# Second self-attention of a Perceiver block: products of whole 128-token tiles, or of 32 by 32 blocks

## The chip, the cores and the metric

The kernel runs on one core of one Trainium2 chip. The metric is the device time of one execution in microseconds. The program is straight-line code for five engines, which meet through semaphores: PE (matmul), DVE (vector), ACT (scalar), POOL (GpSimd) and SP, which issues most of the DMAs.

## The reference, cut to what matters

Six stages follow each other on x of shape (32 batches, 32 tokens, 256 channels): cross-attention, a compressed self-attention with a Fourier transform, a mixture of experts, and the same three once more with other formulas. The change touches stage five, the second self-attention. It has no weights; q, k and v are all the layer-normed x:

```python
def _L1_attn_ref(x):
    qkv = x.reshape(B, S, H, hd).transpose(0, 2, 1, 3)      # H = 16 heads of hd = 16
    q = k = v = qkv
    w = jnp.einsum('bhqd,bhkd->bhqk', q, k) / jnp.sqrt(jnp.asarray(hd, x.dtype))
    w = jnp.where(causal[None, None, :, :], w, mask_value)
    w = jax.nn.softmax(w, axis=-1)
    return jnp.einsum('bhqk,bhkd->bhqd', w, v).transpose(0, 2, 1, 3).reshape(B, S, D)
x = x + _L1_attn_ref(_layernorm(x, axis=-1))
```

A token attends to the tokens of its own batch up to itself, 32 at most.

## The kernel before

The 1024 tokens are eight tiles (`NT`) of 128 partitions, and a tile holds four batches (`QB`) of 32 tokens (`T`). For the self-attention the layer norm (L1459) writes into `xpad`, where each head has 32 columns (`PAD`): its 16 channels, a column of ones, and 15 zeros, which POOL sets ahead (L2098, L2099). Because q and k are the same, the product matrix of a head is symmetric.

For tile n the engines do this. PE transposes xpad, four transposes of four heads (`turn`, L960), into one PSUM bank (t % 2). ACT (even tiles, L1355) or DVE (odd tiles, L1771) copies it to `xpadT`, where head 4r+g is at partitions 32g to 32g+31, block r. PE multiplies each head's 32 x 128 slice with itself (`products`, L973): 16 matmuls, 128 keys by 128 tokens, into the four banks of `upper`, one bank for each g. ACT exponentiates a bank at a time into `gram` (L1365, four instructions). DVE multiplies the pieces g = 0 and 2, and POOL the pieces 1 and 3, by `keep`, which is one where key and token are of the same batch and the key isn't later (L1793, L2106): three quarters of each matrix are other batches' products, set to zero here. PE weighs (`weigh`, L983): 16 matmuls over all 128 keys, with xpad as the stationary operand, which gives channels by tokens in bank 2; the column of ones gives the sum of the exponentials. ACT copies that to `gout` (L1372), PE transposes it back into bank 3 (`turn_back`, L992), and DVE takes the reciprocal of the sums (L1778), scales (L1779), adds to x (L1782) and takes the statistics for the next layer norm (L1437).

The order on each engine is the order of the text; there is no planner. PE's loop is: turn(n+2), products(n+1), turn_back(n-1), weigh(n). `gram`, `gout` and `mixed` have two buffers each, `upper` has one, banks 2 and 3 one each. `after(engine, semaphore, value)` is a wait that is left out for values up to zero.

The stage is written out for all eight tiles, without a loop at run time. The cross-attention before it has one (`slots`, L524): its eight slots are repeated. After the stage, `ln(5)` and `turn_xn(5)` (L574) prepare the experts, whose router matmuls are L1015; the weights of the experts are fetched once the routing is known (L452 to L456).

A float32 matmul shows in the profile as two loads of the stationary operand (PEld) and two MATMULs (PE); a transpose as one of each.

Of the kernel before, what the change touches and what calls it, by code (L numbers as in the profile page):

```python
# [44 lines left out]
C_IDENT, C_SAME, C_PAIR, C_HM1, C_HM16 = 0, 128, 160, 162, 170  # L45
C_CS, C_BD, C_KEEP, C_EVEN, C_RQ, C_RK = 178, 1202, 1458, 1586, 1588, 1620
C_IOTA = C_RK + 32 * (KW2 + 1)
# [15 lines left out]
HG = 3  # L63
KQ = QB * NKEY

V_BQ, V_BK, V_BV, V_CB, V_BO, V_NK, V_NV = 0, 2, 4, 6, 8, 10, 12
# [3 lines left out]
def shape_constants():  # L70
# [21 lines left out]
    q = (p % T)[:, None]  # L92
    c[:, C_KEEP:C_KEEP + P] = (p[:, None] // T == p[None] // T) & (p[:, None] <= p[None])

# [45 lines left out]
def perceiver_block(nc, io, out):  # L140
    ctx = ExitStack()
    with ctx:
# [203 lines left out]
        xpadT = ar.take(GH, TOK)  # L346
        gram = [[ar.take(GH, P) for _ in range(2)] for _ in range(4)]
        gout = [ar.take(GH, P) for _ in range(2)]
        mixed = [ar.take(NH, HD) for _ in range(2)]
        keep = const[:, C_KEEP:C_KEEP + P]  # L350

# [212 lines left out]
        def _(pe):  # L564
# [383 lines left out]
            def self_gram():  # L948
                q = selfs[1]

                def turn(t):

                    if t >= NT:
                        return
                    pe.wait_ge(ln_norm, 4 * NT + t + 1)
                    if t == 0:
                        pe.wait_ge(q["pads"], 1)
                    after(pe, q["turnc" if t % 2 == 0 else "turnd"], t // 2)
                    for r in range(GH):
                        ins = nc.tensor.transpose(bank[t % 2][:, r * P:r * P + P],  # L960
                                                  xpad[:, t, 4 * r:4 * r + 4, :].rearrange("p h d -> p (h d)"), ident)
                    ins.then_inc(q["turnw"], 1)

                def products(n):

                    if n >= NT:
                        return
                    pe.wait_ge(q["turnc" if n % 2 == 0 else "turnd"], n // 2 + 1)
                    after(pe, q["exp"], 4 * n)
                    for r in range(GH):  # L970
                        for g in range(4):
                            v = xpadT[PAD * g:PAD * g + PAD, r, n * P:n * P + P]
                            ins = mm(upper[:, g, r * P:r * P + P], v, v, start=True, stop=True)  # L973
                    ins.then_inc(q["sw"], 1)

                def weigh(n):

                    pe.wait_ge(q["keptv"], 2 * n + 2)
                    pe.wait_ge(q["keptg"], 2 * n + 2)
                    after(pe, q["outc"], n)  # L980
                    for r in range(GH):
                        for g in range(4):
                            ins = mm(bank[2][PAD * g:PAD * g + PAD, r * P:r * P + P], xpad[:, n, 4 * r + g, :],  # L983
                                     gram[g][n % 2][:, r, :], start=True, stop=True)
                    ins.then_inc(q["pvw"], 1)

                def turn_back(n):

                    pe.wait_ge(q["outc"], n + 1)
                    after(pe, q["normed"], n)  # L990
                    for r in range(GH):
                        ins = nc.tensor.transpose(bank[3][:, r * P:r * P + P], gout[n % 2][:, r, :], ident)  # L992
                    ins.then_inc(q["backw"], 1)

                turn(0)
                turn(1)
                products(0)
                for n in range(NT):
                    turn(n + 2)
                    products(n + 1)  # L1000
                    if n:
                        turn_back(n - 1)
                    weigh(n)
                turn_back(NT - 1)

# [103 lines left out]
        def _(act):  # L1109
# [237 lines left out]
            def self_gram():  # L1347
# [9 lines left out]

                def exps(n, g):

                    if n >= NT:  # L1360
                        return
                    act.wait_ge(q["sw"], n + 1)
                    after(act, q["pvw"], n - 1)

                    A(gram[g][n % 2].rearrange("p r q -> p (r q)"), upper[:, g, :], ACT.Exp, scale=HD ** -0.5)\  # L1365
                        .then_inc(q["exp"], 1)

                def weighed(n):

                    act.wait_ge(q["pvw"], n + 1)  # L1370
                    after(act, q["backw"], n - 1)
                    A(gout[n % 2].rearrange("p r q -> p (r q)"), bank[2][:, :], copy).then_inc(q["outc"], 1)  # L1372

                turned(0)
                for g in range(4):
                    exps(0, g)
                for n in range(NT):
                    if n % 2 == 0:
                        turned(n + 2)
                    for g in range(4):  # L1380
                        exps(n + 1, g)
                    weighed(n)

# [43 lines left out]
        def _(dve):  # L1427
# [335 lines left out]
            def self_gram():  # L1763
                q = selfs[1]

                def turned(t):

                    if t >= NT:
                        return
                    dve.wait_ge(q["turnw"], t + 1)  # L1770
                    V.tensor_copy(xpadT[:, :, t * P:t * P + P], bank[t % 2][:, :].rearrange("p (r q) -> p r q", q=P))\  # L1771
                     .then_inc(q["turnd"], 1)

                def norm(n):

                    dve.wait_ge(q["backw"], n + 1)
                    o = bank[3][:, :].rearrange("p (h e) -> p h e", e=PAD)
                    mine(V.reciprocal(srcp[:, :], o[:, :, HD]))  # L1778
# [8 lines left out]

                turned(1)
                for n in range(NT):
                    for g in (0, 2):  # L1790
                        dve.wait_ge(q["exp"], 4 * n + g + 1)
                        v = gram[g][n % 2]
                        V.tensor_tensor(v, v, keep.unsqueeze(1).to_broadcast([P, GH, P]), ALU.mult).then_inc(q["keptv"], 1)  # L1793
                    if n % 2 == 0:
                        turned(n + 3)
                    if n:
                        norm(n - 1)
# [171 lines left out]
        def _(pool):  # L1969
# [125 lines left out]
            def self_gram():  # L2095
# [79 lines left out]
```

## Time and profile before

| | us |
|---|---|
| median of 3 runs (lowest, highest) | 1092.13 (1090.56, 1094.88) |
| the profiled execution, its own time | 1092.83 |
| its span | 1091.0 |
| PE busy / PEld busy | 938.4 / 757.0 |
| DVE / ACT / POOL busy | 548.6 / 466.8 / 340.6 |
| mean granted clock of PE | 0.924 |

The span runs from the first to the last instruction. PE is the matmuls, PEld the weight loads, which overlap them. The page cuts the span into 40 slices of 27 us; the second self-attention lies in slices 32 and 33 counted from 1 (859.9 to 905.1 us). The granted clock is 1.0 at 2.4 GHz and 0.5 at 1.2 GHz.

### The profile page before, as it was taken

Reading aid. Unit: us, or ns where it says so; the run is one execution under the profiler, and the core shown is the slowest. Engines: PE = TensorE matmul, PEld = TensorE weight load, DVE = VectorE, ACT = ScalarE, POOL = GpSimd, SP = SyncE. Lnnn points to the kernel's source line nnn. Section 1 sums busy time; section 2 is a strip of 40 time slices with the busy share of each in tenths; the row PEclk is TensorE's granted clock in tenths of the full one; section 3 lists DMA queues with packets and bytes.
Section 4 is the critical chain, followed back from the end, with each engine's and each line's share of the span. In section 5 each row is a group of like instructions: output and inputs, shape, how many; then the busy total and the mean of one; then the engine's idle time right before and its main releaser. Section 6 shows DMA issues by size and latency. Waiting matters only on the chain.

```text
span 1091.0 us, 24374 instructions
## 1 busy us (share of the span) xinstructions
PE 938.4 (86%) x8690; PEld 757.0 (69%) x8690; DVE 548.6 (50%) x1690; ACT 466.8 (43%) x1374; POOL 340.6 (31%) x388
## 2 busy tenths in 40 slices
PE   5899999979888679999996688999988674799993
PEld 3677777744465469999985466777766453699993
DVE  3666565540264621111117779777776475333334
ACT  2677677742322222332323376777766452011110
POOL 2321112000110141111122468878885250511111
PEclk9899999988898689999996799999999787899997
DMA  8211118000000089888835011111000000899984
GB/s 252 77 40 41 41 39 249 22 1 1 0 1 1 25 304 336 324 323 325 336 120 176 1 40 40 41 41 40 0 1 2 2 2 1 296 322 341 332 324 131
DMA packets 49155, 136.03 MB, mean 125 GB/s; under 512 B 15976, under 2 KB 35696, under 8 KB 43056
## 3 DMA queue, kind: packets, MB, share of 16 engines
q1 hardware_dynamic: 45328, 124.67, 33.0%
q0 software_dynamic: 3744, 10.26, 2.5%
q8 instruction: 51, 0.84, 0.3%
q14 instruction: 32, 0.26, 0.1%
HBM read 117.54 MB, written 17.38 MB: 124 GB/s over the span
## 4 chain that ended last, share of the span: by engine, by line
PE 66%; DVE 16%; POOL 6%; issue 5%; DMA 3%; ACT 2%; SPq 2%; DVEq 0%; POOLq 0%; ACTq 0%
PE lower L1065 14%; PE upper L1076 11%; PE upper L631 7%; PE upper L660 7%; PE upper L696 5%; POOL xslot L2117 3%; PE lower L682 3%; PE upper L713 3%; PE upper L838 2%; PE upper L733 1%; DVE x L1950 1%; PE upper L642 1%; POOL arena L1987 1%; PE lower L883 1%; SPq L428 1%
## 5 line engine op out<-in xcount | busy, mean ns | idle before, releaser
L1065 PEld LDWEIGHTS lower<-arena 128*128 128x128 f32 x1472 | 171.7, 192 | 6.3 <-issue 2.2
L1065 PE MATMUL lower<-arena 128*128 128x128 f32 x1472 | 172.6, 276 | 2.6 <-DMA arena<-in_b_dram 1.2
L1076 PE MATMUL upper<-arena 128*128 128x256 f32 x552 | 130.5, 388 | 0.0
L2123 POOL DMA_INDIRECT ytok<-arena,dest x46 | 44.0, 957 | 257.2 <-DVE arena L1912 235.6
L660 PE MATMUL upper<-wkv,arena 128*128 128x256 f32 x512 | 121.5, 379 | 0.0
L1076 PEld LDWEIGHTS upper<-arena 128*128 128x128 f32 x552 | 104.3, 195 | 13.0
L660 PEld LDWEIGHTS upper<-wkv,arena 128*128 128x128 f32 x512 | 94.3, 191 | 11.3
L1404 ACT ACTIVATE arena<-lower,arena 128x128 f32<-128x128 f32 x184 | 52.5, 369 | 114.2 <-PE lower L1065 114.2
L696 PE MATMUL upper<-const,arena 128*128 128x128 f32 x512 | 80.1, 279 | 6.4 <-ACT arena L1209 6.2
L631 PE MATMUL upper<-wkv,arena 128*128 128x256 f32 x256 | 73.1, 421 | 8.2 <-ACT arena L1146 4.5
L696 PEld LDWEIGHTS upper<-const,arena 128*128 128x128 f32 x512 | 59.6, 142 | 28.2 <-issue 12.6
L2019 POOL TENSOR_TENSOR arena<-arena 128x512 f32<-128x512 f32 x64 | 67.6, 1068 | 14.3 <-DMA arena<-in_ctxT_dram 14.2
L1199 ACT ACTIVATE arena<-arena 128x257 f32<-128x257 f32 x128 | 63.2, 498 | 2.4 <-DVE arena L1486 2.4
L2025 POOL TENSOR_TENSOR arena<-qT,const 128x256 f32<-128x256 f32 x32 | 22.9, 720 | 130.3 <-PE lower L682 114.0
L631 PE MATMUL upper<-arena,wkv 128*128 128x257 f32 x256 | 62.7, 389 | 0.6 <-ACT vlast L1132 0.6
L1410 ACT ACTIVATE arena<-lower 128x512 f32<-128x512 f32 x23 | 13.7, 597 | 114.0 <-PE lower L1065 114.0
L631 PEld LDWEIGHTS upper<-wkv,arena 128*128 128x128 f32 x256 | 49.5, 208 | 17.5 <-ACT arena L1146 4.9
L1199 ACT ACTIVATE arena<-lower,arena 128x257 f32<-128x257 f32 x128 | 59.0, 480 | 5.8 <-DVE arena L1488 5.8
L1900 DVE COPY arena<-lower 128x256 f32<-128x256 f32 x42 | 17.7, 420 | 85.1 <-PE lower L1049 85.1
L2117 POOL DMA_INDIRECT xslot<-arena,slot x32 | 31.9, 996 | 90.6 <-DVE tile_expert L1881 54.9
L1912 DVE COPY arena<-upper 128x256 f32<-128x256 f32 x46 | 19.5, 425 | 74.7 <-PE upper L1076 74.7
L1515 DVE TENSOR_TENSOR arena<-upper,arena 128x128 f32<-128x128 f32 x64 | 18.5, 289 | 75.4 <-ACT arena L1217 75.4
(250 smaller groups left out, 1763.0 us busy)
## 6 DMA issues: line engine op xcount, KB each, us to landing
arena<-in_ew_dram SPq DMA_DIRECT2D x23, 2048.0 KB
arena<-in_ew_dram SPq DMA_DIRECT2D x23, 1536.0 KB
arena<-in_ctxT_dram SPq DMA_DIRECT2D x16, 1028.0 KB, 5.1
xslot<-zero SPq DMA_DIRECT2D x2, 2967.0 KB, 18.8
arena<-xslot SPq DMA_DIRECT2D x46, 129.0 KB
xn<-ytok SPq DMA_DIRECT2D x8, 256.0 KB, 3.9
outT<-ytok SPq DMA_DIRECT2D x8, 256.0 KB, 4.7
const<-in_const_dram SPq DMA_DIRECT2D x1, 1158.0 KB, 7.6
```

The lines of the kernel that those rows point to most:

```text
L631: ins = mm(o, a, v, start=(c == 0), stop=(c == KC - 1))
L660: ins = mm(bank[6 + w][:, 0:D], dctx[k2][:, c, j2, w * P:w * P + P], wkv[l][:, c, D:2 * D], start=(c == 0), stop=(c == KC - 1))
L682: ins = mm(bank[i][64 * c:64 * c + 64, 0:S], xq[k2][rows, c, j2, :, :].rearrange("p e q -> p (e q)"), ktb[j2 % 2][rows, c, :], start=True, ...
L696: ins = nc.tensor.transpose(bank[4][:, i * P:i * P + P], prob[j % 2][:, i, w * P:w * P + P], ident)
L713: mm(bank[5][32 * i:32 * i + 32, 64 * c:64 * c + 64], vb[j % 2][:, w, c * P + 32 * i:c * P + 32 * i + 32], probT[j % 2][:, w, i, 64 * c:64 ...
L1065: ins = mm(bank[1 + half][:, i * P:i * P + P], ew[k][:, at:at + P], exT[k % 2][:, c, :], start=(c == 0), stop=(c == KC - 1))
L1076: ins = mm(bank[4 + k % 2][:, 0:D], eh[k % 2][:, i, :], ew[k][:, at:at + D], start=(i == 0), stop=(i == nh - 1))
L1199: A(prob[j2 % 2][:, i, :], src, ACT.Exp, bias=negmax[j2 % 2][:, i:i + 1], accum_out=rowsum[j2 % 2][:, i:i + 1]).then_inc(q["probs"], 1)
L1404: ins = A(eh[k % 2][:, c, :], bank[1 + half][:, i * P:i * P + P], ACT.Gelu_apprx_tanh, bias=eb1[k][:, c:c + 1])
L2019: G.tensor_tensor(dctx[k2][:, :, j2, :], of[:, :, 0:LASTKEY], of[:, :, LASTKEY:S].to_broadcast([P, KC, LASTKEY]), ALU.subtract).then_inc(q ...
L2117: G.indirect_dma_start(out=xslot[l], out_offset=at(i, t), in_=xrow[:, t, :], in_offset=None)\
L2123: G.indirect_dma_start(out=ytok[l], out_offset=bass.IndirectOffsetOnAxis(ap=dest[k][:, 0:1], axis=0), in_=eys[k], in_offset=None).then_inc ...
```

## The change

Products are made for a batch's own 32 by 32 block only, so that a head and a batch are one matmul with 32 rows and 32 columns of the array; row group g and column group b are the tile of the array that it uses. All 16 heads' blocks of a tile of tokens are 128 partitions by 512 elements, in the first 128 columns of the four banks. One exponential and one mask product take them all, and the mask only has to be causal (32 columns wide). The weighing has the exponentials as stationary operand and xpad as the moving one, 17 columns (`HW`), with head h of batch b at partitions 32b of bank 2 + n % 2: keys are summed and tokens come out on the partitions, so that the copy and the transpose back are gone. ACT makes all copies of the transposes; POOL has no part in the tiles.

```diff
-C_CS, C_BD, C_KEEP, C_EVEN, C_RQ, C_RK = 178, 1202, 1458, 1586, 1588, 1620
+C_CS, C_BD, C_KEEP, C_EVEN, C_RQ, C_RK = 178, 1202, 1458, 1490, 1492, 1524
...
+HW = HD + 1
...
-    c[:, C_KEEP:C_KEEP + P] = (p[:, None] // T == p[None] // T) & (p[:, None] <= p[None])
+    c[:, C_KEEP:C_KEEP + T] = q <= np.arange(T)[None]
...
-        gram = [[ar.take(GH, P) for _ in range(2)] for _ in range(4)]
-        gout = [ar.take(GH, P) for _ in range(2)]
+        gram = [ar.take(4, GH, T) for _ in range(2)]
...
 # PE
-                    after(pe, q["turnc" if t % 2 == 0 else "turnd"], t // 2)
+                    after(pe, q["turnc"], t - 1)
...
-                    after(pe, q["exp"], 4 * n)
+                    pe.wait_ge(q["turnc"], n + 1)
+                    after(pe, q["exp"], n)
                     for r in range(GH):
                         for g in range(4):
-                            v = xpadT[PAD * g:PAD * g + PAD, r, n * P:n * P + P]
-                            ins = mm(upper[:, g, r * P:r * P + P], v, v, start=True, stop=True)
+                            for b in range(QB):
+                                v = xpadT[PAD * g:PAD * g + PAD, r, n * P + T * b:n * P + T * b + T]
+                                ins = mm(upper[T * b:T * b + T, g, T * r:T * r + T], v, v, start=True, stop=True)
                     ins.then_inc(q["sw"], 1)
 
                 def weigh(n):
-                    pe.wait_ge(q["keptv"], 2 * n + 2)
-                    pe.wait_ge(q["keptg"], 2 * n + 2)
-                    after(pe, q["outc"], n)
-                    for r in range(GH):
-                        for g in range(4):
-                            ins = mm(bank[2][PAD * g:PAD * g + PAD, r * P:r * P + P], xpad[:, n, 4 * r + g, :],
-                                     gram[g][n % 2][:, r, :], start=True, stop=True)
+                    pe.wait_ge(q["kept"], n + 1)
+                    after(pe, q["normed"], n - 1)
+                    for h in range(NH):
+                        for b in range(QB):
+                            mine = slice(T * b, T * b + T)
+                            ins = mm(bank[2 + n % 2][mine, HW * h:HW * h + HW], gram[n % 2][mine, h % 4, h // 4, :],
+                                     xpad[mine, n, h, 0:HW], start=True, stop=True)
                     ins.then_inc(q["pvw"], 1)
-                def turn_back(n):
...
 # ACT
-                def exps(n, g):
+                def exps(n):
...
-                    A(gram[g][n % 2].rearrange("p r q -> p (r q)"), upper[:, g, :], ACT.Exp, scale=HD ** -0.5)\
+                    A(gram[n % 2].rearrange("p g r q -> p g (r q)"), upper[:, :, 0:P], ACT.Exp, scale=HD ** -0.5)\
                         .then_inc(q["exp"], 1)
-                def weighed(n):
...
                 turned(0)
-                for g in range(4):
-                    exps(0, g)
+                turned(1)
+                exps(0)
                 for n in range(NT):
-                    if n % 2 == 0:
-                        turned(n + 2)
-                    for g in range(4):
-                        exps(n + 1, g)
-                    weighed(n)
+                    turned(n + 2)
+                    exps(n + 1)
...
 # DVE
+                def kept(n):
+                    dve.wait_ge(q["exp"], n + 1)
+                    v = gram[n % 2].rearrange("p g r q -> p (g r) q")
+                    V.tensor_tensor(v, v, keep.unsqueeze(1).to_broadcast([P, NH, T]), ALU.mult).then_inc(q["kept"], 1)
...
                 for n in range(NT):
-                    for g in (0, 2):
-                        dve.wait_ge(q["exp"], 4 * n + g + 1)
-                        v = gram[g][n % 2]
-                        V.tensor_tensor(v, v, keep.unsqueeze(1).to_broadcast([P, GH, P]), ALU.mult).then_inc(q["keptv"], 1)
-                    if n % 2 == 0:
-                        turned(n + 3)
+                    kept(n)
                     if n:
                         norm(n - 1)
...
 # POOL
-                for n in range(NT):
-                    for g in (1, 3):
-                        pool.wait_ge(q["exp"], 4 * n + g + 1)
-                        v = gram[g][n % 2]
-                        G.tensor_tensor(v, v, keep.unsqueeze(1).to_broadcast([P, GH, P]), ALU.mult).then_inc(q["keptg"], 1)
```

PE's loop becomes turn(n+2), products(n+1), weigh(n). DVE's `norm` waits for `pvw` and reads bank 2 + n % 2 with 17 columns per head; it is otherwise the same.

## Rows read from the trace of the kernel before

**Rows 1.** Busy time by engine (instructions), clock, DMA share and GB/s, over the stage.
```profile
859.90:905.10 45.20, 32.95 (x576) 25.91 (x576) 30.46 (x58) 26.00 (x46) 19.59 (x16) 0.85 0.01 2
```
**Rows 2.** Groups of instructions in the stage: busy us, mean ns, idle before and releaser.
```profile
L2106 POOL TENSOR_TENSOR arena<-arena,const 128x512 f32<-128x512 f32 x16 | 19.6, 1244 | 21.5 <-ACT arena L1365 21.5
L1365 ACT ACTIVATE arena<-upper 128x512 f32<-128x512 f32 x32 | 16.5, 602 | 9.0 <-PE upper L973 9.0
L1793 DVE TENSOR_TENSOR arena<-arena,const 128x512 f32<-128x512 f32 x16 | 13.5, 881 | 2.0 <-ACT arena L1365 2.0
L973 PE MATMUL upper<-arena 32*128 32x128 f32 x256 | 12.2, 341 | 1.7 <-ACT arena L1365 1.7
L983 PE MATMUL lower<-arena 128*32 128x128 f32 x256 | 9.7, 296 | 7.1 <-DVE arena L1793 6.7 <-POOL arena L2106 0.3
L1372 ACT ACTIVATE arena<-lower 128x512 f32<-128x512 f32 x8 | 4.8, 598 | 8.3 <-PE lower L983 8.2
L1771 DVE COPY arena<-lower 128x512 f32<-128x512 f32 x4 | 2.8, 690 | 9.4 <-PE lower L960 9.4
```
**Rows 3.** Timeline of the stage's first and last instructions: start us, us, what.
```profile
859.93 1.97 PE L960 MATMUL lower<-const,arena 128*128 128x128 f32 x8 [3.45 <-DVE arena L1459]
861.08 0.60 ACT L1355 ACTIVATE arena<-lower 128x512 f32<-128x512 f32 x1 [1.89 <-PE lower L960]
861.70 1.28 ACT L1365 ACT_TABLE_LOAD   x1
861.83 1.96 PE L973 MATMUL upper<-arena 32*128 32x128 f32 x32
864.50 0.69 DVE L1793 TENSOR_TENSOR arena<-arena,const 128x512 f32<-128x512 f32 x1 [1.76 <-ACT arena L1365]
...
903.90 0.26 DVE L1778 RECIPROCAL srcp<-lower 128x16 f32<-128x16 f32 x1 [1.00 <-PE lower L992]
904.20 0.42 DVE L1779 TENSOR_TENSOR arena<-lower,srcp 128x256 f32<-128x256 f32 x1
904.65 0.42 DVE L1782 TENSOR_TENSOR x<-x,arena 128x256 f32<-128x256 f32 x1
905.11 0.43 DVE L1437 BATCH_NORM_STATS2 ln_stats<-x 128x6 f32<-128x256 f32 x1
```
**Rows 4.** Chain that ended last, around tile 3: start us, us, what.
```profile
880.42 2.10 DVE arena L1793 x2
882.52 0.04 issue
882.56 1.08 PE lower L983 x32
```
**Rows 5.** Timeline of one burst of small matmuls in the cross-attention.
```profile
851.62 0.52 PEld L713 LDWEIGHTS upper<-arena 128*32 128x32 f32 x32 [2.03 <-issue]
851.65 0.65 PE L713 MATMUL upper<-arena 128*32 128x64 f32 x32 [1.66 <-DVE arena L1507]
```
**Rows 6.** DMA queues (packets, MB, share): the stage; a run-time loop's first pass, 694.9 to 750.4.
```profile
q8 instruction: 5, 0.08, 0.9%
...
q1 hardware_dynamic: 544, 2.11, 11.0%
q8 instruction: 6, 0.10, 0.7%
```
**Rows 7.** That loop: busy times of both passes, then the second pass's only DMA queue.
```profile
694.90:750.40 55.50, 53.47 (x691) 41.59 (x683) 43.36 (x90) 39.87 (x138) 45.20 (x53) 1.00 0.12 40
750.60:805.80 55.20, 53.42 (x683) 41.48 (x676) 42.46 (x90) 39.70 (x137) 45.71 (x53) 1.00 0.06 19
...
q1 hardware_dynamic: 272, 1.05, 5.9%
```
**Rows 8.** A small DMA: issues, KB each, median us from issue to landing.
```profile
negmask<-in_mask_dram SPq DMA_DIRECT2D x4, 32.1 KB, 1.9
```
**Rows 9.** Router matmuls L1015 at either clock: stretch, PE busy, PEld busy, clock.
```profile
912.40:914.60 2.20, 2.20 (x22) 2.20 (x21) 1.00 0.00 0
914.90:916.50 1.60, 1.60 (x8) 1.51 (x8) 0.50 0.00 0
```

More of the change, by code:

```diff
@@ L346, in perceiver_block @@
         xpadT = ar.take(GH, TOK)
-        gram = [[ar.take(GH, P) for _ in range(2)] for _ in range(4)]
-        gout = [ar.take(GH, P) for _ in range(2)]
+        gram = [ar.take(4, GH, T) for _ in range(2)]
         mixed = [ar.take(NH, HD) for _ in range(2)]
-        keep = const[:, C_KEEP:C_KEEP + P]
+        keep = const[:, C_KEEP:C_KEEP + T]
         ar = Arena()
@@ L967, in products @@
                         return
-                    pe.wait_ge(q["turnc" if n % 2 == 0 else "turnd"], n // 2 + 1)
-                    after(pe, q["exp"], 4 * n)
+                    pe.wait_ge(q["turnc"], n + 1)
+                    after(pe, q["exp"], n)
                     for r in range(GH):
                         for g in range(4):
-                            v = xpadT[PAD * g:PAD * g + PAD, r, n * P:n * P + P]
-                            ins = mm(upper[:, g, r * P:r * P + P], v, v, start=True, stop=True)
+                            for b in range(QB):
+                                v = xpadT[PAD * g:PAD * g + PAD, r, n * P + T * b:n * P + T * b + T]
+                                ins = mm(upper[T * b:T * b + T, g, T * r:T * r + T], v, v, start=True, stop=True)
                     ins.then_inc(q["sw"], 1)
                 def weigh(n):
-                    pe.wait_ge(q["keptv"], 2 * n + 2)
-                    pe.wait_ge(q["keptg"], 2 * n + 2)
-                    after(pe, q["outc"], n)
-                    for r in range(GH):
-                        for g in range(4):
-                            ins = mm(bank[2][PAD * g:PAD * g + PAD, r * P:r * P + P], xpad[:, n, 4 * r + g, :],
-                                     gram[g][n % 2][:, r, :], start=True, stop=True)
-                    ins.then_inc(q["pvw"], 1)
-                def turn_back(n):
[L989 to L993, printed above, removed]
+                    pe.wait_ge(q["kept"], n + 1)
[5 more added lines that the diff above has]
+                                     xpad[mine, n, h, 0:HW], start=True, stop=True)
+                    ins.then_inc(q["pvw"], 1)
                 turn(0)
@@ L1000, in self_gram @@
                     products(n + 1)
-                    if n:
-                        turn_back(n - 1)
                     weigh(n)
-                turn_back(NT - 1)
             def experts(l, s):
@@ L1363, in exps @@
                     after(act, q["pvw"], n - 1)
-                    A(gram[g][n % 2].rearrange("p r q -> p (r q)"), upper[:, g, :], ACT.Exp, scale=HD ** -0.5)\
+                    A(gram[n % 2].rearrange("p g r q -> p g (r q)"), upper[:, :, 0:P], ACT.Exp, scale=HD ** -0.5)\
                         .then_inc(q["exp"], 1)
-                def weighed(n):
-                    act.wait_ge(q["pvw"], n + 1)
-                    after(act, q["backw"], n - 1)
-                    A(gout[n % 2].rearrange("p r q -> p (r q)"), bank[2][:, :], copy).then_inc(q["outc"], 1)
                 turned(0)
-                for g in range(4):
-                    exps(0, g)
+                turned(1)
+                exps(0)
                 for n in range(NT):
-                    if n % 2 == 0:
-                        turned(n + 2)
-                    for g in range(4):
-                        exps(n + 1, g)
-                    weighed(n)
+                    turned(n + 2)
+                    exps(n + 1)
             def experts(l):
@@ L1764, in self_gram @@
                 q = selfs[1]
[L1766 to L1772, printed above, removed]
+                def kept(n):
+                    dve.wait_ge(q["exp"], n + 1)
+                    v = gram[n % 2].rearrange("p g r q -> p (g r) q")
+                    V.tensor_tensor(v, v, keep.unsqueeze(1).to_broadcast([P, NH, T]), ALU.mult).then_inc(q["kept"], 1)
                 def norm(n):
-                    dve.wait_ge(q["backw"], n + 1)
-                    o = bank[3][:, :].rearrange("p (h e) -> p h e", e=PAD)
+                    dve.wait_ge(q["pvw"], n + 1)
+                    o = bank[2 + n % 2][:, 0:NH * HW].rearrange("p (h e) -> p h e", e=HW)
                     mine(V.reciprocal(srcp[:, :], o[:, :, HD]))
@@ L1786, in norm @@
                         stats(n)
-                turned(1)
                 for n in range(NT):
-                    for g in (0, 2):
-                        dve.wait_ge(q["exp"], 4 * n + g + 1)
-                        v = gram[g][n % 2]
-                        V.tensor_tensor(v, v, keep.unsqueeze(1).to_broadcast([P, GH, P]), ALU.mult).then_inc(q["keptv"], 1)
-                    if n % 2 == 0:
-                        turned(n + 3)
+                    kept(n)
                     if n:
```

## The prediction

> **What bounds the kernel now.** I read the slices of the page first, then the busy times of the stretch of the second self-attention, its groups of instructions, its chain of waits, and last the instruction queue of the DMA view. The stage runs from the first transposes at 859.93 us to the last addition into x, which ends at 905.07 us [rows 1, 3]: 45.1 us of a span of 1091.0. In it no engine is full: PE is busy 33.0 of 45.2 us, DVE 30.5, ACT 26.0, POOL 19.6 [rows 1]. The reader is to see a ring, not one bottleneck. For a tile of 128 tokens PE writes the 128 by 128 products, ACT exponentiates 16 heads by 128 keys in four pieces of 602 ns, DVE and POOL multiply two pieces each by the keep mask (881 and 1244 ns), PE weighs, ACT copies (598 ns), PE transposes back, DVE divides and adds [rows 2]. The chain passes through the mask products (2.10 us for two), then the weighing (1.08 us) [rows 4]. Most idle time of PE ahead of the weighing, 6.7 us, ends with the DVE mask [rows 2].
>
> **What the change does, part by part.** The sum is made against the profiled execution, 1092.83 us with a span of 1091.0; the median of the timed runs is 0.7 us lower, and I give the forecast for the median.
>
> ACT: 32 exponentials of 128x512 become 8 of the same 512 elements, 24 x 0.60 = 14.4 us less; eight copies L1372 go (4.8 us); four copies move over from DVE (+2.4 us). ACT then has 8 copies and 8 exponentials, 1.2 us per tile [rows 2].
> DVE: 16 masks become 8 of the same form, the four copies L1771 go. Per tile there remain one mask (0.69 us alone, [rows 3]) and the division, addition and statistics, 0.26+0.42+0.42+0.43 us with gaps, about 1.6: 2.3 us [rows 3].
> POOL: all 16 masks go (19.6 us), and with them the stretching of DVE's mask from 0.69 to 0.88 us. POOL's queue holds only two memsets and the flag ahead of the stage, so nothing else moves.
> PE: the 32 transposes back go. Transposes in stay, 0.58 us per tile from start to start of what follows. Products were 16 matmuls per tile and are 64; weighing was 16 and is 64. Each matmul here is two loads and two MATMULs: L973 has 256 of each for 8 tiles of 16 [rows 2]. So a tile now issues 2 x 128 loads and 2 x 128 MATMULs. With the transposes, one pair each, it is 72 pairs before (4+32+32+4) and 260 after.
> The const load is 49 KB smaller of 1158, at most 0.2 us of the start; I cost it at nothing.
>
> How long does PE take for 128 pairs? The trace has no 32x32 tiles. The nearest rows are 32 pairs of 128x32 with 64 columns in 0.65 us, loads starting over 0.52 less one load of 0.11: one pair per 13 ns, though each takes 216 ns [rows 5]. Small tiles beside each other thus do overlap, four at a time. With the same pace 128 pairs take 1.7 us; with shorter streams (32 and 17 columns) the pairs could start twice as fast, 0.85 us. I take 1.1 us, the end and the switch of shape included, for each of the two. PE's work per tile is then 0.58+1.1+1.1 = 2.8 us, above ACT's 1.2 and DVE's 2.3. The ring closes in time: from the end of products, exponential 0.6, mask 0.7, both beside the previous tile's weighing and the next transposes (1.7 us). Were this all, the first weighing would end at 866.6 (the exponential waits for the table load and one copy, until 864.2, then PE still has products 1 and weighing 0), the last products at 866.6+1.7+5x2.8-0.6 = 881.7 (no transposes are left for the last two), and exponential, mask, weighing and the last division and addition would follow by 886: 19 us saved.
>
> **The step that I think takes most of it back: instruction loading.** 8 x 260 pairs are 4160 loads and MATMULs in place of 1152. They come from memory over q8 in packets of 16 KB: 5 packets for the stage's 576+576 [rows 1, 6]; 6 for the first pass of a loop with 691+683, and none in its second pass [rows 6, 7]. That is about 230 loads and MATMULs each; with the waits, which the counts leave out, I take 250 instructions per packet. The stage then needs 16.6 packets: one already there, and 16 in turn. A packet takes 0.9% of 16 engines over 45.2 us in five, 1.3 us each [rows 6]. How far ahead they are asked for no row shows directly. But a loop of six packets was still there in the second pass, so whatever is buffered must leave room for what lies behind, and little need lie ahead. I assume one ahead: the next packet is asked for when the one before is entered. No stretch of the trace uses packets faster than one per 6 us, so it hides this wholly.
>
> The period P of packets in a row is the 1.3 us plus the time from asking to the start. Bounds: 1.3 us when that is nothing or when several are under way (then the 1.4 us per packet of PE's own pace bind), and 1.3+1.9 = 3.2 when it is as long as the whole of a small transfer, 1.9 us from issue to landing for 32 KB [rows 8]. I take 1.0 for it, about the middle: P = 2.3. The first packet is asked for as the products start, 861.8 [rows 3]; it and 15 more land by 861.8+16P; then half a microsecond of instructions and 1.2 us for the last division and addition [rows 3]: the stage ends at 863.6+16P = 900.4. Saved: 905.1-900.4 = 4.7 us. At P = 2.0 it is 9.5, at 2.6 nothing, at 3.2 minus 9.7.
>
> After the stage all is shifted: layer norm, routing, and the expert stage, whose weights are asked for only once the routing is known. One thing differs. Router matmuls L1015 now run mostly at the full clock, 22 in 2.2 us; at half clock 8 take 1.6 [rows 9]. If PE, idle half the time in the new stage, comes out at 1.2 GHz, up to 24 x 0.1 = 2.4 us go; I take 0.6. Within the stage half clock is covered by P: transposes 1.2, weighing perhaps 1.8 and products 1.2 are below 2P.
>
> Sum: 1092.8-4.7+0.6 = 1088.7 profiled, **1088** for the median. ±0.5% (5.5 us) is what a measurement of this kernel can tell from no change.
>
> The Trainium skill bears on this in two places. "Runtime: NRT & Kernel Launch", section Instruction fetch mechanics, has the sequencer fetch the next 16 KiB block while it executes the current one and calls the cost mostly hidden, and gives PE room for 2048 instructions. The block size agrees with 0.08 MB in 5 packets. If that room were kept filled ahead, seven packets would be there at the start, the other nine would come within 9 x 2.3 = 21 us, and the first rival below would hold; a room of eight that keeps a loop of six or seven leaves one ahead, and my forecast holds.
>
> **Rivals.**
> First, loading is not what binds (asked for further ahead, or several at once). Then 886 for the end and, with a little cold clock, 1092.1-19+1 = 1074. For it: a loaded program never stalls in this trace; packets come smoothly. Against: the memory of the loop argument, and no stretch that needs more than one in 6 us.
> Second, on the other side: from asking to landing costs as much as a small transfer on top of the packet, P = 2.8 to 3.2. The point from which it decides is P = 2.6. At 3.2 the stage ends at 914.8: 1092.1+9.7+0.6 = 1102.
> Third, also slower: the small tiles do not run side by side in the weighing. There four row groups write one PSUM bank, while in the products (as in L973 before, four row groups of 32) each group has its own. If a tile's pairs ran one at a time at the 55 ns that a column tile takes between its own (13 ns x 4, [rows 5]), weighing costs 128 x 0.055 = 7 us per tile, the tile 8.7 us, the stage 8 x 8.7 and some 5 at its ends, 75 in place of 45: 1122. No row shows it either way; four column tiles of one row group do share a bank at L713. "TensorEngine Tiling (Array Packing)" of the Trainium skill, section Restrictions and Gotchas, says that different row tiles cannot access the same PSUM bank simultaneously, which speaks for this rival; here they write disjoint partitions, which speaks against.
>
> **How the numbers follow.** Forecast (P from 2.0 to 2.8) 0.47, its own range 1083 to 1096; loading not binding 0.28; P above 2.8 0.15; weighing one at a time 0.10. Faster by over 0.5% means below 1086.6: all of the first rival and the part of the forecast with P below about 2.2, 0.28+0.14 = 0.42. Slower means above 1097.6: most of the second rival and the third, 0.24. The rest, 0.34, is the same. The range goes from the first rival to the end of the second, 1073 to 1102, and leaves out the third and little else.
>
> **What would show it.** Right: q8 has 16 or 17 packets in the stage, nearly evenly spaced by 2.0 to 2.8 us, with PE's idle time put down to issue and not to ACT or DVE; a burst of products or weighing is broken in the middle, about every 250 instructions; the stage takes 36 to 46 us; POOL is empty; ACT has 8 exponentials of 0.60 us. Wrong: PE waits named by DVE or ACT with packets bunched at the front (first rival), or weighing pairs 50 ns apart without packets missing (third). If products take less than 0.8 us or more than 1.7 where no packet is late, my pace of pairs was off, which matters only under the first rival.

## The result, and the profile after

The changed kernel takes 1108.83 us (1105.29 to 1111.36, 4 runs) against 1091.37 for the kernel before on the same chip: ratio 1.0151, 95% interval 1.0114 to 1.0189. It is slower by 1.5%, and outside the range that was given. The profiled execution took 1111.36 us with a span of 1109.5, 18.5 us more than before.

Busy times, clock and DMA over the stage, from the first transposes to the last addition into x; then its groups of instructions (line, busy us, mean ns, idle before and its releaser):

```profile
859.90:921.40 61.50, 37.41 (x2080) 32.69 (x2080) 19.87 (x47) 12.12 (x18) 0.00 (x0) 0.50 0.02 5
```
```profile
L984 PE MATMUL lower<-arena 32*32 32x17 f32 x1024 | 17.1, 211 | 14.9 <-issue 14.9
L974 PE MATMUL upper<-arena 32*32 32x32 f32 x1024 | 14.0, 245 | 6.7 <-issue 6.5 <-ACT arena L1355 0.2
L1751 DVE TENSOR_TENSOR arena<-arena,const 128x512 f32<-128x512 f32 x8 | 5.5, 692 | 21.2 <-ACT arena L1355 21.2
L1345 ACT ACTIVATE arena<-lower 128x512 f32<-128x512 f32 x8 | 4.8, 598 | 24.6 <-PE lower L960 24.6
L1355 ACT ACTIVATE arena<-upper 128x512 f32<-128x512 f32 x8 | 4.8, 597 | 18.3 <-PE upper L974 18.2
```

Against [rows 1, 2], ACT fell from 26.0 to 12.1 us, DVE from 30.5 to 19.9 and POOL from 19.6 to nothing. PE gained only 4.5 us of busy time for 1504 more matmuls, yet the stage grew from 45.1 to 61.2 us, by 16.0. PE's idle time says why: 21.4 us of it ahead of products and weighing ends with "issue", where PE waited for nothing that the profile shows, and almost none with ACT or DVE. The timeline shows where it lies (start us, us, instruction, idle before); a matmul that follows such idle time is called a restart here:

```profile
869.28 1.58 PE L984 MATMUL lower<-arena 32*32 32x17 f32 x104 [2.14 <-issue]
870.79 1.11 PE L960 MATMUL lower<-const,arena 128*128 128x128 f32 x4
871.84 0.37 PE L974 MATMUL upper<-arena 32*32 32x32 f32 x19
872.70 1.33 PE L974 MATMUL upper<-arena 32*32 32x32 f32 x106 [0.50 <-issue]
...
876.16 1.68 PE L984 MATMUL lower<-arena 32*32 32x17 f32 x109 [1.87 <-issue]
877.77 1.11 PE L960 MATMUL lower<-const,arena 128*128 128x128 f32 x4
878.81 0.35 PE L974 MATMUL upper<-arena 32*32 32x32 f32 x14
879.86 1.42 PE L974 MATMUL upper<-arena 32*32 32x32 f32 x114 [0.70 <-issue]
...
919.86 0.18 PEld L984 LDWEIGHTS lower<-arena 32*32 32x32 f32 x4 [1.92 <-issue]
...
920.95 0.42 DVE L1761 TENSOR_TENSOR x<-x,arena 128x256 f32<-128x256 f32 x1
```

Both bursts are broken in the middle, where the program has no wait. From one break to the next PE runs 104+4+19 = 127 and then 109+4+14 = 127 pairs of a load and a matmul (between them, in the rows shown and left out, 128), that is 254 instructions plus the waits. And from one restart to the next it is the same 3.4 to 3.7 us: 869.28, 872.70, 876.16, 879.86; to 919.86 it is fourteen such periods of **3.61 us**. The DMA view of 869.2 to 881.2 us in 40 slices of 0.3 us shows the packets themselves, and the same view of the stage counts them:

```profile
GB/s 0 0 0 0 55 0 0 0 0 0 0 0 0 0 0 55 0 0 0 0 0 0 0 0 0 0 55 0 0 0 0 0 0 0 0 0 0 0 0 55
...
q8 instruction: 17, 0.28, 1.9%
```

They start at 870.4, 873.7, 877.0 and 880.9 (each to within 0.3 us), 0.8 to 1.4 us behind a restart, and PE restarts 2 to 3 us behind each of them. The spacing stays the same whether PE then works for 2.9 us (869.28 to 872.2) or for 1.6 (872.70 to 874.3). That fits a next block which is asked for when PE enters the one before it, with only one under way. Of the seventeen packets the last one starts behind the last restart of 919.86 us and belongs to what follows the stage; the other sixteen are the 16 of the prediction.

The rest of the difference stands behind the stage. The clock is at half (0.50) in the whole stage, where before had 0.85, and stays there into the router (before, then after; PE busy, mean ns):

```profile
L1015 PE MATMUL upper<-rw,xnT 128*128 128x8 f32 x32 | 4.5, 282 | 0.7 <-ACT xnT L1120 0.7
```
```profile
L1005 PE MATMUL upper<-rw,xnT 128*128 128x8 f32 x32 | 7.0, 362 | 0.7 <-ACT xnT L1110 0.7
```

The sum: the stage begins 0.3 us later than before's, at 860.18 us, and takes 16.0 us more, so that the last addition ends at 921.37 us instead of 905.07 [rows 3], 16.3 us later. The router's matmuls take 2.5 us longer. Together that is 18.8 us, and the span grew by 18.5.

### The profile page after: what moved, and what is told of

It reads as the page before. It is cut to its first block, busy times and chain, and to the rows that moved or that the text cites. A ratio compares the mean times of both kernels' runs of the same rounds, so it can differ in the third digit from the quotient of the medians.

```text
span 1109.5 us, 27293 instructions
## 1 busy us (share of the span) xinstructions
PE 942.2 (85%) x10194; PEld 764.1 (69%) x10194; DVE 537.6 (48%) x1678; ACT 452.7 (41%) x1346; POOL 321.6 (29%) x372
## 4 chain that ended last, share of the span: by engine, by line
PE 67%; DVE 13%; issue 7%; POOL 6%; DMA 3%; ACT 2%; SPq 2%; DVEq 0%; POOLq 0%; ACTq 0%
PE lower L1055 14%; PE upper L1066 11%; PE upper L631 7%; PE upper L660 7%; PE upper L696 5%; POOL xslot L2084 3%; PE lower L682 3%; PE upper L713 3%; PE upper L838 2%; PE upper L733 1%; PE lower L984 1%; DVE x L1923 1%; PE upper L642 1%; PE lower L883 1%; POOL arena L1960 1%
## 5 line engine op out<-in xcount | busy, mean ns | idle before, releaser
L696 PEld LDWEIGHTS upper<-const,arena 128*128 128x128 f32 x512 | 59.6, 142 | 28.2 <-issue 12.6
L1496 DVE TENSOR_TENSOR arena<-upper,arena 128x128 f32<-128x128 f32 x64 | 18.5, 289 | 75.9 <-ACT arena L1207 75.9
## 6 DMA issues: line engine op xcount, KB each, us to landing
xslot<-zero SPq DMA_DIRECT2D x2, 2967.0 KB, 18.8
```

The lines of the kernel that those rows point to most:

```text
L696: ins = nc.tensor.transpose(bank[4][:, i * P:i * P + P], prob[j % 2][:, i, w * P:w * P + P], ident)
```

## The experiments

Each was timed beside the kernel before on the same chip, whose median was 1092.64 for e1 to e4, 1092.05 for e5 to e8, 1094.09 for e9 to e11 and 1094.51 for e12. "Stage" runs from the first transposes to the end of the last addition into x in the profiled execution. The first transposes start up to 3 us earlier or later than in after, though no edit is aimed at the work ahead of them, so the stages are compared by their lengths. "Clock" is the mean granted clock of that stretch; "packets" are those of q8 in it, and for the loops (e3, e7, e8, e10, e11) those of a stretch of whole passes behind the first. Instructions are loads, matmuls and transposes, without waits; "kept" means that a run-time loop repeats them.

| kernel | instructions a tile | packets | clock | stage, from to (length) us | median us | ratio to before, 95% |
|---|---|---|---|---|---|---|
| before | 144 | 5 | 0.85 | 859.93 to 905.07 (45.1) | 1091.37 | 1 |
| after | 520 | 17 | 0.50 | 860.18 to 921.37 (61.2) | 1108.83 | 1.0151 [1.0114, 1.0189] |
| e1 before, both split | 528 | 17 | 0.92 | 859.20 to 925.74 (66.5) | 1114.09 | 1.0207 [1.0156, 1.0259] |
| e2 before, weighing split | 336 | 11 | 0.88 | 858.65 to 914.41 (55.8) | 1103.07 | 1.0113 [1.0066, 1.0159] |
| e3 loop | 522, kept | 0 | 0.50 | 858.24 to 915.01 (56.8) | 1105.07 | 1.0130 [1.0082, 1.0178] |
| e4 whole products | 328 | 11 | 0.61 | 860.62 to 905.86 (45.2) | 1092.68 | 1.0016 [0.9989, 1.0044] |
| e5 half weighing | 392 | 13 | 0.50 | 858.66 to 907.03 (48.4) | 1096.21 | 1.0033 [1.0015, 1.0051] |
| e6 three fillers | 532 | 17 | 0.79 | 861.27 to 931.19 (69.9) | 1118.20 | 1.0218 [1.0176, 1.0260] |
| e7 loop, mask apart | 522, kept | 0 | 0.50 | 857.71 to 905.04 (47.3) | 1095.55 | 1.0039 [1.0015, 1.0063] |
| e8 e7, two fillers | 530, kept | 0 | 0.85 | 859.92 to 913.37 (53.5) | 1103.49 | 1.0093 [1.0057, 1.0128] |
| e9 one filler | 524 | 17 | 0.50 | 858.39 to 921.03 (62.6) | 1112.72 | 1.0184 [1.0136, 1.0231] |
| e10 e7, 512 columns | 526, kept | 0 | 0.50 | 863.08 to 924.75 (61.7) | 1108.95 | 1.0113 [1.0043, 1.0184] |
| e11 e7, 256 columns | 526, kept | 0 | 0.50 | 859.11 to 913.26 (54.2) | 1103.37 | 1.0115 [1.0050, 1.0179] |
| e12 blocks of 64 | 264 | 9 | 0.54 | 857.86 to 905.49 (47.6) | 1095.03 | 1.0002 [0.9982, 1.0023] |

**Are the instructions enough to lose the time?** e1 leaves the kernel before its tiles, masks and copies, and only cuts its matmuls in four; e2 cuts the weighing alone.

```diff
-ins = mm(upper[:, g, r * P:r * P + P], v, v, start=True, stop=True)
+for b in range(QB):
+    ins = mm(upper[T * b:T * b + T, g, r * P:r * P + P], v[:, T * b:T * b + T], v, start=True, stop=True)
```
```diff
-ins = mm(bank[2][PAD * g:PAD * g + PAD, r * P:r * P + P], xpad[:, n, 4 * r + g, :],
-         gram[g][n % 2][:, r, :], start=True, stop=True)
+for b in range(QB):
+    ins = mm(bank[2][PAD * g:PAD * g + PAD, r * P + T * b:r * P + T * b + T], xpad[:, n, 4 * r + g, :],
+             gram[g][n % 2][:, r, T * b:T * b + T], start=True, stop=True)
```

> The kernel before with the same work for ACT, DVE and POOL, the same copies and the same result, but every products matmul cut into four by its stationary columns (32 of 128) and every weighing matmul cut into four by its moving columns: 264 pairs of load and MATMUL per tile in place of 72. Theory (instruction packets of 256 instructions come one at a time, 3.65 us each, when PE has nothing else to do): 528 instructions are 2.1 packets, 7.6 us per tile against 5.6 before, so the stage takes 61 to 64 us in place of 45 and the kernel 1107 to 1111 us. Rival A (the change is slow because of its own shapes, 32x32 stationary blocks with 32 or 17 moving columns, or of row groups that share a bank): these stay out of it, so about the time of before, 1091 to 1095. Rival B (half clock alone): like before unless PE falls to 1.2 GHz.

> The same with only the weighing cut into four: 168 pairs, 336 instructions per tile, 1.3 packets. Theory: 1.3 x 3.65 = 4.8 us of loading per tile lies below the 5.6 us that the tile takes anyway, so the loading is mostly hidden: 1091 to 1096 us, far less than half of what the full cut costs. If cost simply followed the number of matmuls (a fixed price for each), it would be half of the full cut, some 1099 to 1101.

e1 came out 3 us above what was expected. PE's timeline in e1, then in e2:

```profile
880.25 2.34 PE L974 MATMUL upper<-arena 32*32 32x128 f32 x128
882.51 0.66 PE L995 MATMUL lower<-const,arena 128*128 128x128 f32 x4
883.10 0.31 PE L986 MATMUL lower<-arena 128*32 128x32 f32 x4
884.15 2.04 PE L986 MATMUL lower<-arena 128*32 128x32 f32 x97 [0.74 <-issue]
```
```profile
875.90 1.17 PE L973 MATMUL upper<-arena 32*128 32x128 f32 x32
877.00 0.65 PE L993 MATMUL lower<-const,arena 128*128 128x128 f32 x4
877.59 2.74 PE L984 MATMUL lower<-arena 128*32 128x32 f32 x128
```

e1 has the broken bursts of after at full clock, and its 17 packets start 3.8 us apart on average: the breaks don't come from a slow clock. But it isn't loading alone: e2 missed, and shows why. Its bursts are whole, and its stage is 10.6 us longer than before's all the same, because 128 pairs with 128 rows take 2.74 us where 32 took 1.08 [rows 4]. A split matmul costs PE time too, and in e1 both costs are mixed. A cleaner test changes the instructions of after.

**Fewer instructions, more work.** e5 takes a quarter of the instructions out of after by not weighing the heads 8 to 15, whose results are then not the kernel's; e6 and e9 put TensorE work in with hardly any instructions.

```diff
-for h in range(NH):          # weigh(n) of after
+for h in range(NH // 2):     # e5
...
+mm(bank[2 + n % 2][:, 0:4 * P], ident, const[:, 0:4 * P], start=True, stop=True)   # e9, in weigh(n); e6 also in turn and products
```

> The kernel after with the weighing of heads 8 to 15 left out: 64 pairs and 128 instructions fewer a tile (392 instead of 520), waits and buffers as they are. Theory A (the tile costs as long as its instruction packets: one for 256 instructions, one every 3.61 us in the stage of after, the next asked for only when the block ahead is entered): 1.53 packets a tile by 3.61 us is 5.5 us in place of 2.03 by 3.61 = 7.3; eight tiles give back about 14 us: 1094 to 1098 us, with stalls at block boundaries still in every tile. Rival (PE's own work at half clock sets the tile, loading only rides along): 64 weighing pairs at 15 ns are 0.95 us a tile, 8 us in all: about 1101 us. If something else sets the tile (exponential, mask, division): within 3 us of after, 1106 or more.

> The kernel after with three extra matmuls of 128x128 by 512 columns a tile, one in each of the steps that turn, multiply and weigh, into banks that the step overwrites. They are 6 instructions and some 1.9 us of TensorE work a tile (128x512 f32 rows: 0.59 to 0.69 us each), 15 us over the stage. Theory A (loading sets the tile; TensorE stalls about 1.8 us at each of two boundaries a tile): the added work fits into the stalls. If the granted clock then stays at full, the router's 31 matmuls (6.8 us at half clock) get their 2.3 us back: 1105 to 1110 us, the stage within 2 us of after. Rival B (the half clock over the stage is the cause): at full clock the tile shortens by more than the stalls hide: 1095 to 1102 us. Rival C (TensorE's work adds up): 1118 to 1124 us.

> e6 added more TensorE work than I had reckoned: one filler of 512 columns took 0.95 us from start to start at full clock and 1.84 at half, three of them 2.85 to 5.5 us a tile against stalls of about 3.5. Here is one filler a tile, in the weighing. Theory A (loading sets the tile of after): the filler lies in the stalls, the stage keeps its packet period of 3.6 to 3.75 us and stays within 2 us of after's; if the clock stays full behind it the router gets 2.3 us back: 1106 to 1110 us. Rival C (TensorE's work adds up): 8 times 0.95 to 1.84 more, 1116 to 1123 us. Rival B (the half clock sets the tile of after): with full clock below 1102 us.

e5 hit: 12.8 us less of stage and 12.6 us less of time than after's median. Its bursts still break every 128 pairs (PE timeline):

```profile
874.65 0.35 PE L974 MATMUL upper<-arena 32*32 32x32 f32 x14
876.01 1.41 PE L974 MATMUL upper<-arena 32*32 32x32 f32 x114 [1.01 <-issue]
877.21 0.41 PE L984 MATMUL lower<-arena 32*32 32x17 f32 x14
879.85 0.92 PE L984 MATMUL lower<-arena 32*32 32x17 f32 x50 [2.24 <-issue]
```

What it leaves out would have been 64 x 15 ns a tile, 7.7 us in all, were PE's own pace the limit. e6 landed in the range of its rival C, that the work adds up: the stage grew by 8.7 us. It doesn't decide between loading and work, since a filler costs 0.95 us at full clock and 1.84 at half where I had reckoned 0.63, and three of them a tile are more than the stalls hide. e9 is the clear one. The filler's group, and the stage:

```profile
L981 PE MATMUL lower<-const 128*128 128x512 f32 x16 | 16.6, 1141 | 0.0
...
L985 PE MATMUL lower<-arena 32*32 32x17 f32 x1024 | 15.8, 211 | 0.7 <-issue 0.7
```
```profile
862.00:921.00 59.00, 49.39 (x1960) 33.35 (x1959) 17.34 (x39) 9.94 (x16) 0.00 (x0) 0.50 0.02 4
```

PE is busy 49.4 us in these 59, where after had 35.6 in the same stretch, 13.8 more, and the stage is 1.5 us longer than after's (62.6 against 61.2), within the 2 us that were expected. The rest of the work went into the stalls: the idle time ahead of the weighing fell from 14.9 to 0.7 us. The median missed the expected 1106 to 1110 by 3 us and stayed below the 1116 of rival C; before too was 2.7 us higher beside it, and the intervals of the two ratios overlap.

**No loading at all.** e3 keeps one tile's TensorE code in a run-time loop. The matmuls there read fixed buffers, into which GpSimd and ACT copy each tile, and the buffers are single. e7 gives the mask product a buffer of its own.

```diff
+with pe.Fori(1, NT + 1) as it:
+    products(it)
+    for name in ("xt", "kept", "xw", "normed"):
+        pe.wait_ge(q[name], it)
+    turn(xt1)
+    weigh(it)
...
-V.tensor_tensor(v, v, keep.unsqueeze(1).to_broadcast([P, NH, T]), ALU.mult)    # e3: in place, exp waits for weigh
+V.tensor_tensor(v, e, keep.unsqueeze(1).to_broadcast([P, NH, T]), ALU.mult)    # e7: from gramE into gram1
-act.wait_ge(q["pvw"], n + 1)
+act.wait_ge(q["kept"], n + 1)
+dve.wait_ge(q["pvw"], n + 1)                                                  # e7: the mask product waits for weigh instead
```

> The changed kernel with the tile's PE code in a run-time loop: the same 64+64 matmuls and 4 transposes in the same shapes per tile, eight times, but only some 540 instructions of code. PE reads fixed buffers, into which POOL copies the tile of xpad and ACT writes the transpose and the exponentials; buffers are single, one idle weighing and one small transpose per pass are added. Theory: packets of the instruction queue only in the first pass (2 or 3, and one for the weighing after the loop, fetched early); first pass 7 us, each further one 3.5 to 4.5 us with no idle time put down to issue inside a burst; stage 36 to 42 us in place of 60; the kernel 1083 to 1094 us. Rivals A and B (shapes, bank sharing, half clock): every pass stays near 7 us and the kernel at 1105 or above.

> The loop of e3 (one tile's TensorE code kept and run nine times, no packet in the passes) with one chain cut: the mask multiply writes another buffer than the exponential's, so that the exponential of tile n+1 no longer waits for the weighing of tile n. In e3 a pass took 6.10 us, about 4.4 of them the burst and 1.7 the wait for the exponential and the copy behind the weighing. Theory A: 4.9 to 5.3 us a pass without any packet, 8 to 9 us less than e3: 1095 to 1099 us. Rival (the 1.7 us is the loop's own cost, branch and semaphores): 1103 to 1106 us as e3.

From the second pass on there are no packets and no break inside a burst. e3 missed (1105.07 us, at the edge of its rivals' range) since a new wait took their place: the exponential (L1343) waits for the weighing, then the copy (L1338), then the products, here in its timeline:

```profile
877.25 1.91 PE L975 MATMUL lower<-arena 32*32 32x17 f32 x128
...
879.28 0.60 ACT L1343 ACTIVATE arena<-upper 128x512 f32<-128x512 f32 x1 [5.02 <-PE lower L975]
879.77 0.59 ACT L1338 ACTIVATE arena<-lower 128x512 f32<-128x512 f32 x1
...
880.42 0.48 PE L963 MATMUL lower<-const 128*128 128x128 f32 x1 [1.27 <-ACT arena L1338]
```

e7 takes that wait out and hit: PE is busy 33.1 of 34.3 us, a pass takes 4.98 us, and the stage takes 47.3 us, 2.2 more than before's. Its stretch of whole passes, then one pass:

```profile
865.70:900.00 34.30, 33.10 (x1826) 28.32 (x1824) 15.81 (x31) 9.04 (x14) 6.82 (x13) 0.50 0.00 0
```
```profile
875.15 0.44 PE L963 MATMUL lower<-const 128*128 128x128 f32 x1 [0.18 <-issue]
...
875.53 1.54 PE L968 MATMUL upper<-arena 32*32 32x32 f32 x128
...
877.00 1.11 PE L956 MATMUL lower<-const,arena 128*128 128x128 f32 x4
...
878.05 1.91 PE L975 MATMUL lower<-arena 32*32 32x17 f32 x128
...
880.13 0.45 PE L963 MATMUL lower<-const 128*128 128x128 f32 x1 [0.18 <-issue]
```

With one transpose and two copies more a tile, and one weighing more in all, than after, the same pairs take 13.9 us less of stage, at the same half clock. With e5 and e9 this shows that loading is what lengthened the stage. Without it, the half clock is next.

**The half clock.** Fillers in e7's loop were to raise it.

```diff
 nc.tensor.transpose(bank[3][:, 0:P], ident, ident)
+mm(bank[3][:, 0:4 * P], ident, const[:, 0:4 * P], start=True, stop=True)   # e10; e8 a second one ahead of weigh; e11 0:2 * P
```

> e7 with two extra matmuls of 128x128 by 512 columns in each pass, about 1.2 us of TensorE work a pass, to raise the granted clock; no packets in the passes. Theory B (at half clock the pairs are what is left of the loss): at full clock turn, products and weighing shrink from 4.4 to about 3 us and the router gets 2.3 us back: 1088 to 1094 us even with the added work. Rival (the pairs run at a pace of their own whatever the clock, about 12 to 15 ns): the added work adds to the pass: 1102 to 1108 us, less up to 2.3 us at the router.

> e7 with one filler of 512 columns a pass. e8 at full clock took 5.36 us a pass, 1.9 of them two fillers, so that the pass without them is 3.45 us at full clock against 4.98 at half in e7. If one filler holds the full clock from the first passes on: 4.4 us a pass, 4 to 5 us less than e7, 1090 to 1093 us. If the clock stays half: 4.98 + 1.84 = 6.8 us a pass, 1108 to 1112 us. If it rises in the middle of the stage, as in e8: between, near 1100.

> e7 with one filler of 256 columns a pass (about 0.5 us at full clock, 0.95 at half). Full clock: 3.95 us a pass, 8 to 9 us less than e7, 1086 to 1090 us, which would be below before. Half clock: 5.9 us a pass, 1101 to 1105 us.

e8 missed: 1103.49 us in place of 1088 to 1094. Its clock rose only at 874 us, and the two fillers cost more than the clock gave back. Its stretch at full clock, then its weighing and its products:

```profile
874.00:911.00 37.00, 32.97 (x1778) 22.28 (x1777) 17.57 (x35) 8.76 (x14) 7.38 (x13) 1.00 0.00 0
```
```profile
880.47 1.26 PE L976 MATMUL lower<-arena 32*32 32x17 f32 x128
...
883.18 1.29 PE L969 MATMUL upper<-arena 32*32 32x32 f32 x128
```

At 2.4 GHz the weighing takes 1.26 us instead of 1.91, the products 1.29 instead of 1.54, the transposes 0.63 instead of 1.11; a pass is 5.36 us, and about 3.5 less its two fillers of 0.95. But in e10 and e11, with one filler, the clock of the profiled executions stayed at 0.50 over the stage, and the filler's time was added to each pass: both gave the times that were expected for half clock. One run of e10 reached a mean clock of 0.921 and 1099.33 us, the others 0.901 to 0.907 and 1107.5 to 1112.5. I found no way to full clock that costs less than it brings.

**Versions in between.** e4 keeps before's whole products, and exponentiates only the own blocks, in four pieces of 32 partitions; e12 makes the blocks 64 by 64. The removed lines are those of after.

```diff
-for b in range(QB):                                                     # e4
-    v = xpadT[PAD * g:PAD * g + PAD, r, n * P + T * b:n * P + T * b + T]
-    ins = mm(upper[T * b:T * b + T, g, T * r:T * r + T], v, v, start=True, stop=True)
+v = xpadT[PAD * g:PAD * g + PAD, r, n * P:n * P + P]
+ins = mm(upper[:, g, r * P:r * P + P], v, v, start=True, stop=True)
...
+for b in range(2):                                                      # e12
+    v = xpadT[PAD * g:PAD * g + PAD, r, n * P + HB * b:n * P + HB * b + HB]
+    ins = mm(upper[HB * b:HB * b + HB, g, HB * r:HB * r + HB], v, v, start=True, stop=True)
```

> Products as in the kernel before (16 matmuls of 128x128), the exponential only on each batch's own block, four instructions on 32 partitions each, into the small buffer; mask, weighing and division as in the change. 164 pairs, 328 instructions per tile, 1.3 packets. Theory: 1.3 x 3.65 = 4.7 us per tile by loading; ACT 5 x 0.6 = 3.0 us; stage 40 to 44 us, kernel 1087 to 1093. Rival A with the weighing as the slow part (row groups sharing a bank): the weighing is unchanged, so at least half of the loss stays, 1099 and above.

> The change with blocks of 64 by 64 (two batches, with a mask that also drops the other batch's keys) in place of 32 by 32: 64 pairs for the products and 64 for the weighing, 264 instructions and their waits a tile instead of 520; two exponentials of 128x512 a tile, one mask multiply on VectorE and one on GpSimd. Theory A (a packet of 256 instructions every 3.6 to 3.7 us, asked for when the block ahead is entered): 1.03 packets a tile, 3.75 us against 7.04 in after and 4.5 in before; with the first addition at 871 to 872 us as in after, the last comes at 898 to 900, some 6 us before the 905.07 of before. With the router at half clock (2.3 us): 1085 to 1090 us, level with before or under it; at full clock 1083 to 1087. Rival (each pair costs more with more columns and rows, so that TensorE's work of a tile stays above 4.5 us, as the 128 split weighing pairs of e2 took 2.7 us): 1092 to 1098 us.

e4 is level with before, as expected, though four pieces of 32 partitions cost ACT as much as four of 128 (2.42 us). e12 is level too, where 5 to 9 us less were expected; it fell into the range of its rival, that a larger pair costs more. Its bursts are whole; its timeline shows the larger cost:

```profile
885.49 1.29 PE L976 MATMUL upper<-arena 32*64 32x64 f32 x64
...
886.71 3.49 PEld L987 LDWEIGHTS lower<-arena 64*64 64x64 f32 x64
```

64 loads of 64x64 take 3.49 us, 54 ns each, against 14 ns for those of 32x32 (1.80 us for 128) in e7 at the same clock. Half the pairs then cost more than all of them did. Which of size, order or bank does it was not separated. No version here beats the kernel before.

## Why the prediction was wrong

**What bounds before; ACT, DVE, POOL.** Right: eight exponentials of 597 ns, a mask product of 0.69 us, copies at 598 ns, nothing on POOL. None of it was on the path any longer.

**The work of PE.** 260 pairs a tile, as counted. I took 1.1 us for 128 pairs; they took 1.54 and 1.91 at half clock, 1.29 and 1.26 at full. That was too cheap by 0.2 us at full clock and by 0.4 to 0.8 at half, and without effect under loading, as the prediction said.

**Instruction loading.** The mechanism was the right one and its count too: about 250 instructions to a packet, one ahead, 16 in turn, bursts broken mid-way, idle time put down to issue. **The failed step is the size of P**, "P = 2.3" with 3.2 as its upper bound. It was 3.61. Put into the prediction's own formula, 863.6+16P, it gives 921.4; the stage ended at 921.37. So close a match is in part luck: the products started 0.3 us later than assumed, and the end behind the last packet took 1.5 us and not 1.8 (its own two terms give 1.7). I added the time from asking to start to the 1.3 us of the packet and let PE go on the moment it landed. The views show 0.8 to 1.4 us from PE's restart to the packet's start and 2 to 3 us from there to the next restart, well over the packet's own 1.1 us (1.9% of 16 engines over 61.4 us in 17). With about 1.1 us up to the packet's start and 1.1 for the packet, some 1.4 of the 3.61 us lie between landing and running, a leg that the prediction did not have. The "upper bound" was thus no bound: it held two of three parts. The break-even of 2.6 was right, and 3.61 is on the far side of it.

The Trainium skill, "Runtime: NRT & Kernel Launch", section Instruction fetch mechanics, calls the cost of crossing a block mostly hidden. Here that holds for before and not for after, whose stalls are 21.4 us: it depends on how fast PE runs through 256 instructions, and 3.6 us is 14 ns for each of them.

**The clock.** I put 0.6 us on the router and 2.4 as its worst; it was 2.5, since half clock held from the first transposes to the router. In the stage it was covered by P, as forecast: e1 has the same breaks at 0.92, and e9's 13.8 us of extra work at half clock lengthened the stage by 1.5 us.

**The rivals.** "Loading does not bind" (1074) is refuted twice over: loading binds, and e7, which is free of it but has single buffers and one small transpose a pass more, still needs 47.3 us of stage against before's 45.1. Its pass takes 4.98 us at half clock where I had counted 2.8 a tile, and that takes the 19 us that I had counted as saved. The rival of slow loading (1102) was the right one, with 0.15 and a P still too small. The weighing one at a time (1122) didn't come: weighing pairs with four row groups in one bank start about 14 ns apart at half clock (e7) and 9 ns at full (e8), not 55. The rule quoted there from the Trainium skill, "TensorEngine Tiling (Array Packing)", section Restrictions and Gotchas, so didn't make them start one at a time here, where the tiles write disjoint partitions.

## What to carry to other kernels

Count the instructions of a stage as well as its work: where TensorE could run through 256 of them in less than about 3.6 us, that period set the time here, at either clock. Replacing one 128-wide matmul by four small ones, in products and weighing alike, lost more than it saved elsewhere; keeping the products whole (e4) came out level. The sign in a profile is a burst cut in its middle, idle time put down to issue, and evenly spaced packets on the instruction queue. When bounding a round trip, list all its legs (asked, started, landed, used) before calling a sum an upper bound.

## What had not been expected of the hardware

- A block of instructions every 3.61 us at half clock (3.8 in e1, mostly at full), and one ahead only, though a loop of 522 instructions a pass (e3, e7) runs without a packet.
- The stalls of loading hide all but 1.5 us of 13.8 us of added TensorE work (e9).
- Loads of 64x64 one per 54 ns, loads of 32x32 one per 14 ns, at the same half clock (e12, e7).
- In e9, PE busy 49.4 of 59 us, and in e7, 33.1 of 34.3, the granted clock stayed at 1.2 GHz; in e8, with two fillers a pass, it rose to 2.4 within the stage.
- An exponential of 32 partitions by 512 takes as long as one of 128 by 512: four in 2.42 us (e4).
